# One of the 62 gathered columns of every chunk fetched by SyncE, row by row

## What is computed

```
h = max(layernorm(x), 0);  x += L0(h)      # two RGAT convolutions, 4 heads, 8 relations
h = max(layernorm(x), 0);  x += L1(h)      # one GAT convolution
h = max(layernorm(x), 0);  x += L2(h)      # RGCN, 8 relations
h = max(layernorm(x), 0);  x += L3(h)      # GINE: edge features and a small MLP

# every one of the first four does, for each edge e:
out_j = xw[etype[e], src[e]]               # a row of 64 features, gathered
attn  = softmax over the edges of one target of leaky_relu(qn[etype, dst] + kn[etype, src])
agg[dst] += attn * out_j                   # RGCN: the edge's weight instead of attn
```

## Time and profile before

| | |
|---|---|
| device time, median of 3 runs | 22912.39 us (22912.26 to 22913.14) |
| the profiled execution's own time | 22925.71 us |
| its span | 22924.0 us |
| GpSimd busy | 16620.5 us, 73% |
| VectorE busy | 10608.1 us, 46% |
| ScalarE busy | 5400.6 us, 24% |
| TensorE busy (matmul) | 5314.1 us, 23% |
| mean busy share of DMA queues, GpSimd's and SyncE's | 12.9% and 12.6% of 16 engines |

### The profile page before, as it was taken

One profiled execution on the slowest core, in us unless ns is written; L12 is line 12 of the kernel. 1 busy time (PEld: TensorE's weight loads), 2 busy tenths in 40 slices (PEclk: granted clock), 3 DMA queues, 4 the chain that ended last, 5 costly groups with the idle time before them and its releaser, 6 DMA issues.

```text
span 22924.0 us, 117388 instructions
## 1 busy us (share of the span) xinstructions
PE 5314.1 (23%) x30665; PEld 3875.9 (17%) x30665; DVE 10608.1 (46%) x9479; ACT 5400.6 (24%) x4709; POOL 16620.5 (73%) x17277
## 2 busy tenths in 40 slices
PE   2000000010000001222222256666663322222201
PEld 1000000010000001222222245555552000000001
DVE  3443444324444343565665557878875111111167
ACT  1222222222222221111111132222221221112175
POOL 7777777677777776777777767777776777777733
PEclk9999999999999999666666655555555666666655
DMA  5333333332222222222222222121221222222164
GB/s 202 93 100 96 93 102 93 100 89 68 74 68 74 68 68 45 53 56 53 53 56 53 54 85 53 51 55 51 54 52 52 83 78 80 76 76 79 69 230 163
DMA packets 721060, 1832.34 MB, mean 80 GB/s; under 512 B 317342, under 2 KB 351502, under 8 KB 659826
## 3 DMA queue, kind: packets, MB, share of 16 engines
q0 software_dynamic: 550784, 576.42, 12.9%
q1 hardware_dynamic: 133474, 1091.60, 12.6%
q10 hardware_dynamic: 36752, 163.80, 1.8%
HBM read 1007.27 MB, written 929.07 MB: 84 GB/s over the span
## 4 chain that ended last, share of the span: by engine, by line
POOL 67%; issue 24%; PE 3%; DVE 3%; DMA 2%; ACT 1%; POOLq 0%; SPq 0%; DVEq 0%; ACTq 0%
POOL region L635 55%; POOL by_src L721 11%; DMA region<-by_src 2%; PE ps L1156 1%; DVE region L1485 1%; POOL q_rel L692 1%; PE ps L1158 1%; DVE region L1514 1%; PE ps L1117 0%; POOL h_edge L704 0%; POOL q_one L692 0%; PE ps L1119 0%; DMA by_src<-region,idx 0%; ACT region L949 0%; ACT ps L957 0%
## 5 line engine op out<-in xcount | busy, mean ns | idle before, releaser
L635 POOL DMA_INDIRECT region<-table,idx x12896 | 12178.2, 944 | 3996.4 <-issue 3936.1
L721 POOL DMA_INDIRECT by_src<-region,idx x3224 | 3125.9, 970 | 1007.8 <-issue 997.1
L1824 DVE TENSOR_TENSOR region<-ps,region 128x248 f32<-128x248 f32 (+1 forms) x156 | 74.4, 477 | 4324.2 <-DMA region<-table,idx 4324.2
L1778 DVE TENSOR_TENSOR ps<-region,ps 128x1008 f32<-128x1008 f32 x832 | 1577.2, 1918 | 679.5 <-DMA region<-table,idx 574.3
L1165 PE MATMUL ps<-ident,region 128*68 128x128 f32 (+1 forms) x3 | 1.3, 444 | 8114.0 <-DVE region L1925 8114.0
L1781 DVE TENSOR_TENSOR_SCAN region<-region,ps 128x1008 f32<-128x1008 f32 x832 | 1849.9, 2244 | 10.7
L1714 DVE TENSOR_TENSOR region<-ps,region 128x2048 bf16<-128x2048 f32 x833 | 1844.9, 2215 | 14.1
L849 ACT COPY region<-region 128x4216 f32<-128x4216 f32 (+1 forms) x156 | 1182.3, 7579 | 2478.1 <-DVE region L1906 2478.1
L1061 PE MATMUL ps<-region 98*128 98x128 f32 x6448 | 1659.0, 438 | 321.7 <-DVEq L1876 192.6
L1480 DVE CAST region<-src 128x62 f32 (+1 forms) x52 | 11.6, 223 | 3466.9 <-DMA by_src<-region,idx 3466.8
L1156 PE MATMUL ps<-region,ident 128*128 128x512 f32 (+1 forms) x832 | 809.4, 1062 | 3142.3 <-DVE region L1485 3142.3
(11 more groups left out here) (285 smaller groups left out, 15383.2 us busy)
## 6 DMA issues: line engine op xcount, KB each, us to landing
sums<-region SPq DMA_DIRECT2D x104, 2232.0 KB
region<-table,idx POOLq DMA_INDIRECT x12896
sums<-region SPq DMA_DIRECT2D x52, 2046.0 KB
region<-by_src SPq DMA_DIRECT2D x52, 2015.0 KB, 9.6
region<-q_rel SPq DMA_DIRECT2D x104, 992.0 KB
h_edge<-zeros_d SPq DMA_DIRECT2D x52, 1984.0 KB
sums<-region SPq DMA_DIRECT2D x52, 1984.0 KB
region<-h_edge SPq DMA_DIRECT2D x52, 1984.0 KB, 12.3
```

The costliest lines, as they stand in the source:

```text
L635: pool.indirect_dma_start(out=to, out_offset=None, in_=table, in_offset=bass.IndirectOffsetOnAxis(ap=index, axis=0)).then_inc(s, 16)
L721: pool.indirect_dma_start(out=by_src, out_offset=bass.IndirectOffsetOnAxis(ap=idx[:, b, j:j + 1], axis=0), in_=MSG[:, b, j, :], in_offset= ...
L1778: return tt(wg[q % 2].rearrange("p (f j) -> p f j", f=PF), rows, bc(weight[q], 1, PF), ALU.mult)
```

## The change

In each chunk of the four gather passes GpSimd gathers 61 columns (`JP`) and SP fetches the 62nd. SP can't gather by a list in SBUF, so it loads the row numbers into registers, 16 at a time (`RUN`), and issues 128 transfers of one table row each, one for each partition, with the address computed from a register. Their completion is counted on four semaphores a layer (slot and half), for which VectorE waits beside `gathered`.

The row numbers come from two small lists in device memory (`row_lists`: source, and source times 8 plus edge type), written once at the start: SP loads the last column of each chunk of `src` and `edge_type` (52 x 128 single numbers each), VectorE combines them, SP stores them. For every chunk SP then loads one list of 128 into `row_list`.

SP does the chunks 0 and 1 ahead of its loop. In the loop, the 128 transfers for the chunk after the next stand in two halves of 64 around the store of this chunk's sums. To have semaphores for this, the search's 14 semaphores become 4 (`mid_in`, `low_in`), with a wait of GpSimd for the turn before the last, and `iota_in` is folded into `consts`.

```diff
+            sp.dma_start(row_list[:, 1, :], a["src"].rearrange("(p c j) -> c p j", p=P, c=CH)[:, :, J - 1]).then_inc(loaded, 16)
+            sp.dma_start(row_list[:, 0, :],
+                         a["edge_type_8"].rearrange("(p c j) -> c p j", p=P, c=CH)[:, :, J - 1]).then_inc(loaded, 16)
+            indices = [sp.alloc_register(f"row{k}") for k in range(RUN)]
             sp.wait_ge(dst_ready, 1)
             sp.dma_start(dst_f.rearrange("(p s) k -> p (s k)", p=P), dst_v).then_inc(idx_dram, 16)
             sp.dma_start(sub_last, sub_v).then_inc(idx_dram, 16)
+            sp.wait_ge(lists_ready, 1)
+            sp.dma_start(row_lists[0:CH, :], row_list[:, 0, :]).then_inc(list_in, 16)
+            sp.dma_start(row_lists[CH:2 * CH, :], row_list[:, 1, :]).then_inc(list_in, 16)
...
+                def load_list(i, b):
+                    kind = 0 if REL_OF[l] > 1 else CH
+                    at = kind + 2 * i + b if isinstance(i, int) else bass.ds(i * 2 + (kind + b), 1)
+                    here = row_lists[at:at + 1, :] if isinstance(i, int) else row_lists[at, :]
+                    sp.dma_start(row_list[0:1, b, :], here).then_inc(list_in, 16)
+                def fetch_rows(i, b, half):
+                    if half == 0:
+                        load_list(i, b)
+                        sp.wait_ge(idx_ready, i * 2 + ((CH + 2) * l + b + 1))
+                        sp.sem_inc(chunk_begun, 1)
+                        sp.wait_ge(list_in, i * 32 + 16 * (CH * l + b + 3))
+                        sp.sem_inc(chunk_begun, 1)
+                    for p0 in range(half * P // 2, (half + 1) * P // 2, RUN):
+                        sp.load(indices, row_list[0:1, b, p0:p0 + RUN])
+                        for k, row in enumerate([sp.snap(r) for r in indices]):
+                            sp.dma_start(G[p0 + k:p0 + k + 1, b, J, :],
+                                         tables[l][bass.ds(row, 1), :]).then_inc(rows_in[l][b][half], 16)
+                for q in range(GP):
+                    sp.wait_ge(stored[q], 16 * TURNS * (l + 1))
+                if l == CONV1:
+                    sp.wait_ge(list_in, 32)
+                for b in range(2):
+                    fetch_rows(0, b, 0)
+                    fetch_rows(0, b, 1)
-                def chunk_transfers(i, b, more):
+                def chunk_transfers(i, b, more, ahead):
                     if h and more:
                         sp.wait_ge(e_read, i * 2 + (CH * l + b + 1))
                         sp.dma_start(q_to, q_rows[:, bass.ds(i * (2 * w) + (b + 1) * w, w)]).then_inc(e_in, 16)
+                    if ahead:
+                        fetch_rows(i + 1, b, 0)
                     sp.wait_ge(sum_ready, i * 2 + (CH * l + b + 1))
                     sp.dma_start(rows[:, bass.ds(i * (2 * J) + b * J, J), :], O).then_inc(sum_out, 16)
...
+                    if ahead:
+                        fetch_rows(i + 1, b, 1)
...
-                        for j in range(J):
+                        for j in range(JP):
                             gather(G[:, b, 1 + j, :], tables[l], idx[:, b, j:j + 1], gathered[l][b])
...
-                            dve.wait_ge(gathered[l][b], i * (16 * J) + 16 * J)
+                            dve.wait_ge(gathered[l][b], i * (16 * JP) + 16 * JP)
+                            for half in range(2):
+                                dve.wait_ge(rows_in[l][b][half], i * (8 * P) + 8 * P)
```

More of the change, by code:

```diff
@@ L64 @@
 PF = D // PIECES
+JP = J - 1
+RUN = 16
 assert HI * LO == NP and NG % 2 == 0 and NQ == 2 * NG and GROUP == 2 * QUAD and FARTHER > NP
@@ L140, in build @@
         src_ends = dram("src_ends", (2, NP))
+        row_lists = dram("row_lists", (2 * CH, P), I32)
         X = sb("X", [P, NT, D])
@@ L163, in build @@
         edge0 = sb("edge0", [P, 1])
+        row_list = sb("row_list", [CH, 2, P], I32)
         iota_r = sb("iota_r", [P, REL])
@@ L174, in build @@
         st = sb("st", [P, 4, NT])
-        R = 31580
+        R = 31324
         region = sb("region", [P, R])
@@ L325, in build @@
         idx_dram = sem("idx_dram")
-        mid_in = [sem(f"mid_in{g}") for g in range(TURNS)]
-        low_in = [sem(f"low_in{g}") for g in range(TURNS)]
+        mid_in = [sem(f"mid_in{k}") for k in range(2)]
+        low_in = [sem(f"low_in{k}") for k in range(2)]
+        lists_ready = sem("lists_ready")
+        list_in = sem("list_in")
+        rows_in = {l: [[sem(f"rows_in{l}_{b}_{k}") for k in range(2)] for b in range(2)] for l in SUMMED}
         dst_ready = sem("dst_ready")
@@ L575, in _ @@
                 rows = sums[l].rearrange("(p j) f -> p j f", p=P)
-                h, _, O = slots(l)
+                h, G, O = slots(l)
                 if h:
@@ L596, in chunk_transfers @@
                         sp.dma_start(he[:, bass.ds(i * (2 * J * D) + b * J * D, J * D)], zeros_d).then_inc(big_zero, 16)
+                    if ahead:
+                        fetch_rows(i + 1, b, 1)
                 with sp.Fori(0, CH // 2 - 1) as i:
                     for b in range(2):
[L600 to L602 removed]
+                        chunk_transfers(i, b, True, True)
+                chunk_transfers(CH // 2 - 1, 0, True, False)
+                chunk_transfers(CH // 2 - 1, 1, False, False)
             for b in range(2):
@@ L675, in _ @@
                 pool.wait_ge(search, g + 1)
+                if g > 1:
+                    pool.wait_ge(mid_in[g % 2], 16 * GT * (g // 2))
                 for t in range(GT):
-                    gather(got_mid[g][:, t, :], sub_last, ix_i[:, 0, GT * g + t:GT * g + t + 1], mid_in[g])
+                    gather(got_mid[g][:, t, :], sub_last, ix_i[:, 0, GT * g + t:GT * g + t + 1], mid_in[g % 2])
             for g in range(TURNS):
                 pool.wait_ge(search, TURNS + g + 1)
+                if g > 1:
+                    pool.wait_ge(low_in[g % 2], 16 * GT * (g // 2))
                 for t in range(GT):
-                    gather(got_low[g][:, t, :], dst_f, ix_i[:, 1, GT * g + t:GT * g + t + 1], low_in[g])
+                    gather(got_low[g][:, t, :], dst_f, ix_i[:, 1, GT * g + t:GT * g + t + 1], low_in[g % 2])
             pool.wait_ge(index_done, 1)
@@ L1276, in _ @@
             dve.tensor_copy(cont_b, cont_all[:, 0:1].to_broadcast([P, P])).then_inc(top_in, 1)
-            dve.wait_ge(loaded, 16 * 5)
+            dve.wait_ge(loaded, 16 * 7)
+            stt(out=row_list[:, 0, :], in0=row_list[:, 1, :], scalar=float(REL), in1=row_list[:, 0, :], op0=ALU.mult,
+                op1=ALU.add).then_inc(lists_ready, 1)
             done(dve.tensor_copy(rel[:, :], src8[:, 0:EPP]))
@@ L1541, in sorted_sums @@
                 dve.wait_ge(flag_in, CH)
-                dve.wait_ge(iota_in, 1)
+                dve.wait_ge(consts, 7)
                 done(dve.tensor_reduce(cont_all[:, :], cont[:, 0:EPP], AX, ALU.min))
```

7 lines of the change are left out of this document (3 added, 4 removed).

## The result

The changed kernel takes 22946.97 us (median of 20 runs, 22934.65 to 22954.57). The kernel before, run beside it on the same chip, takes 22912.62 us (20 runs, 22897.13 to 22917.38). The ratio is 1.0015 [1.0009, 1.0021]: 34 us more, 0.15%, less than the 0.2% that the prediction counts as a difference. Forecast were 23890 us. The forecast is wrong, and so is the main rival, in which SP keeps up and the kernel comes out at 22703 us.

The account below looks back on a forecast made before the run. GpSimd's gathers were taken to bound the kernel, with SP becoming the pace maker: 331 + 295 + 149 + 123 + 63 + 17 = 978 us more, giving 23890 us (4.3% slower), range 22650 to 26000.

Parts of the forecast that it names:

- SP keeps up: Rival, chance 0.36: a 16-register load takes 0.6 us, GpSimd sets the pace in every pass, 22703 us.
- The gain, 260 us: Four gather passes: 208 gathers fewer at 1.249 us each save 260 us if GpSimd stays the pace maker.
- one row: SP's chunk: register work 0.19 us plus issue 0.29 make 0.48 us a row (bounds 0.48 and 0.59), 61.4 us for 128.
- 8 register loads: SP's chunk: 16 registers a load at 1.6 us, plus 0.2 of register operations, 14.4 us a chunk (bounds 2 and 38).
- SP sets the pace everywhere: Four passes: SP needs 83.8, 83.1, 80.3 and 79.8 us a chunk, above GpSimd's 76.2.
- nothing makes SP wait but its list: Four passes: indices are there long before and the row buffer is free, so SP waits only for its list.
- The ends, 23, 23 and 17 us: Pass ends: last query rows issued behind the last row transfers add 23 us in CONV1 and CONV2, 17 in GAT.
- The store of the sums ... still lands in time: SP's loop: store moves about 40 us later, but ScalarE needs the buffer only 69 us after the old issue; no cost.
- Instruction fetch, 0.9 us a chunk: SP's loop: the 572-instruction body may be fetched anew, 1.7 us a turn, 0.9 us a chunk (bounds 0 and 4).
- The start, 17 us: Kernel start: two loads of 6656 single numbers, 8.3 us each, delay the target list by 17 us (bounds 1 and 50).
- Dear registers: Rival, chance 0.10: registers read one by one at 0.2 us, 3.2 us a load, 2660 us more, 26550 us.
- a full queue: Rival, chance 0.04: row transfers behind 2 MB of sums held at issue, 8 us a chunk, 1660 us more, 25550 us.

Follow-up runs that it names:

- all three orders mended: Changed kernel with RGCN's sums stored ahead of the rows, query rows loaded earlier, start's two list loads behind the stores: 22659.72 us, 0.9887 of the kernel before.
- query rows earlier: Changed kernel with each chunk's query-row load moved behind the first half of the rows, one chunk sooner: 36521.19 us on the slow chip, 22836.47 us (0.9966) on another.

## Why the prediction was wrong, by its own steps

**The gain, 260 us: right.** Without rows the kernel is 251 us faster, with all three orders mended 254 us.

**SP's chunk: the term "one row" was mis-sized, and the size of the forecast failed here.** The four chunks of CONV2 from 6011.79 to 6318.93 (two turns of the loop) give 76.8 us each; I sorted the steps between SP's instructions by kind:

| us a chunk, CONV2 | forecast | measured |
|---|---|---|
| 128 rows | 61.4 (0.48 each) | 54.6 (0.43) |
| 8 register loads | 14.4 (1.6 + 0.2) | 15.1 (1.45 + 0.44) |
| wait for the list | 4.5 | 3.9 |
| turn of the loop, fetch | 0.9 | 1.3 |
| the rest | 1.9 | 1.9 |
| sum | 83.1 | 76.8 |

The load, to which the prediction gave most of its doubt, was within 5%. The row, which it took as nearly known, was off by 6.8 us a chunk. It borrowed the issue of a single number (287 ns), but a row's issue is 225 ns. The 0.19 us that it put between the end of one issue and the next was right: by the median they are 0.18 us (0.41 from row to row less 0.225), of which register operation and move take 0.13. The stated bounds for a row, 0.48 to 0.59 us, didn't hold the value: the lower one was a row of another shape, not a bound. Since SP's chunk lies within 1.5 us of GpSimd's, this one term is more than the whole 4%. With a row at 0.43 us the forecast's own sum has CONV1 at 77.0 us, CONV2 at 76.3 and GAT and RGCN at GpSimd's 76.2, which makes -22 - 59 - 64 - 64, and with 46 for two ends and 17 for the start -146 us: some 22770, faster (an estimate from its own terms). What turns that into a draw is RGCN, below. The sum also doesn't turn at a load of 1.0 us, as the prediction says: with its rows at 0.48 and a load of 1.0 it still gives some 60 us more, and the sign turns at about 0.9.

**"SP sets the pace everywhere": wrong in two passes of four.** In CONV1 SP needs 1.4 us a chunk more than GpSimd, in CONV2 0.4; in GAT it waits for the indices instead (127.1 us in 37 waits between 9260 and 13040), and in RGCN too (360.5 in 49). So "nothing makes SP wait but its list" fails in both. The gap of several us that GpSimd was to have at each chunk is there in RGCN alone, and VectorE starts a chunk of CONV2 every 76.7 us, not 83. The rival "SP keeps up" said that SP isn't what holds the passes up, but from a load of 0.6 us; the load is 1.23, and the cheaper rows paid for it.

**The ends, 23, 23 and 17 us: right in mechanism for the first two.** CONV1 lost 59 us and CONV2 31; GAT, where SP isn't late, nothing. I read CONV1's as 23 for the query rows and the rest from SP's lateness of a pass, which the forecast counted in the pace; this division is worked out and not measured by a run of its own. Of 50 x 1.4 = 70 us of it, 22 show up as longer gathering, 36 at the end, and some 13 are what SP was ahead at first (its first query rows at 585.8, GpSimd's third chunk at 446.9 + 152.4 = 599.3).

**"The store of the sums ... still lands in time": wrong, and of what was measured this cost most.** The forecast looked at when ScalarE needs the buffer again in CONV2, 69 us later, and carried that to all passes. In RGCN ScalarE wants it before SP has even issued the store (13.37 us of waiting end at 15079.86, so from 15066.49; the issue is at 15073.22), and what then follows makes the next indices, for which SP waits before it starts the rows ahead of the next store. The ring by the rows above: indices to rows 2.2 us, half the rows and the issue 32.0, landing 6.6, copies and scans to the next indices 38.6 (to 15118.42): 79.35 us, where the kernel of before had 77.43. It loses 152 us of gathering and 17 at the end; moving the store back returned both. That RGCN came out close to its forecast (+104 us where 123 was forecast, a chunk of 79.35 where 79.8 was) is luck: forecast was SP busy for the whole chunk, and SP idles 7.4 us of it.

**Instruction fetch, 0.9 us a chunk: right that it comes, more than that in all.** The step back to the head of SP's loop takes 2.6 us a turn, 1.3 a chunk, and 0.25 us a turn where the kernel leaves the rows out. Besides, some steps inside are long: the mean row is 0.43 us with a median of 0.41, the mean load 1.45 with a median of 1.26. I read these as fetches too, since the packets added are some 8.7 for each turn of the loop; that part is argued, no run separates it. The Trainium skill, "Runtime: NRT & Kernel Launch", "Instruction fetch mechanics", says that a taken branch outside a small window stalls for a fetch; the loop's step of 2.6 us agrees.

**The start, 17 us: right in mechanism, half the size.** The loads were issued in 2.16 and 4.16 us, not 8.3 each, but then held the next issue for 4.21 us where it took 1.98. The first gather starts at 40.5 instead of 32.1. Why SP is held that long at some issues, no run shows.

**Dear registers and a full queue: neither.** The first would have needed 3.2 us a load. The same section of the Trainium skill gives about 200 ns a register for loads from device memory; here a load of 16 from SBUF takes 1.23 us, 77 ns a register, and one more register costs 57 ns, so the measurement decides against it for a load from SBUF. Rows behind a store of the sums keep their 225 ns: SP's rows of the second half took 32.92 us for 64, those of the first 31.82.

## What to carry to other kernels

When an engine's queue is handed work that by its sum comes within a few per cent of the pace maker, the sum isn't the forecast: write down what stands behind the new work in that in-order queue and who waits for each of it, in every pass and not only in the one that was read, since such places and the start ate some 290 us here, and three moves gave nearly all of it back. Put a small load that is waited for ahead of a large one, and the last consumer's data ahead of the bulk. And a price borrowed from a row of another shape is one end of a guess, not a bound, above all where it is multiplied by 26,624.

## What the runs showed of the hardware

- SP can fetch single rows addressed from registers at 0.41 us each (issue 225 ns), with 16 addresses read from SBUF in 1.23 us (8 in 0.775 us): 0.54 us a row in all in CONV2 (54.6 + 15.1 us for 128). GpSimd's gather of 128 rows is 1.25 us.
- SP's loop body of 572 instructions is fetched anew: 904 instruction packets, 7.41 MB, instead of 37 (243 with rows in one pass, 676 in three, 38 with none), and 2.6 us at the branch back instead of 0.16 (0.25 with no rows).
- A list issued on the same queue behind 992 KB of query rows is waited for 3.8 us, without them 0.9 us.
- Two loads of 6656 single numbers held their queue for 2.16 and 4.16 us at issue, and the next issue for 4.21 us; placed last they took 1.00 and 7.50 us.
- One chip took 29669.36 us for the kernel before (9 runs), where others take 22912 and 22957. There a row's issue has the same median, 225 ns, but moves of 29 ns took up to 1.46 us (line 618, query rows earlier), and the change, even in its best version, lost 22%. What differs on that chip is open.
